# A two-layer graph attention kernel: three PSUM banks for the edge sums, scores two groups behind, softmax one slot later

## What is computed

```
def _egat_conv(x, e, src, dst, W_ni, W_nj, W_fij, W_node, attn):
    f = (x @ W_ni.T)[src] + (x @ W_nj.T)[dst] + e @ W_fij.T
    f = leaky_relu(f, negative_slope=0.2)
    score = f @ attn
    m = segment_max(score, dst)
    a = exp(score - m[dst])
    a = a / segment_sum(a, dst)[dst]
    h = x @ W_node.T
    return segment_sum(h[src] * a[:, None], dst), f

h0, h1 = _egat_conv(x, e, src, dst, ...W1...)
h0 = relu(h0) + x
h1 = relu(h1) + e
h0b, _ = _egat_conv(h0, h1, src, dst, ...W2...)
out = layernorm(x + h0b + x)
```

## Time and profile before

| what | us |
|---|---|
| median of 3 runs | 2160.43 (2159.26 to 2163.89) |
| the profiled execution | 2163.74 |
| its span, first to last instruction | 2162.0 |
| PE busy | 1872.9 (87%) |
| POOL busy | 1593.5 (74%) |
| DVE busy | 1351.5 (63%) |
| ACT busy | 672.6 (31%) |

### The profile page before, as it was taken

How to read it: one execution, slowest core, us unless ns; L and a number is a source line. 1 busy time by engine, 2 the same in 40 slices (tenths; PEclk the granted TensorE clock), 3 DMA queues, 4 the chain that set the end, 5 groups by cost and what they waited for, 6 DMA issues and landing times.

```text
span 2162.0 us, 41030 instructions
## 1 busy us (share of the span) xinstructions
PE 1872.9 (87%) x10816; PEld 1284.3 (59%) x10816; DVE 1351.5 (63%) x4574; ACT 672.6 (31%) x1260; POOL 1593.5 (74%) x1664
## 2 busy tenths in 40 slices
PE   5799999898888899898978998888888888888887
PEld 4366766566565666566756666565555555565656
DVE  6477776665665666665745756656556556555655
ACT  2555444443433434443211112222222222122221
POOL 7777777777777777777577777777777777777771
PEclk9899999989999989988989989989999999989998
DMA  9888898888888888888756776666766766766761
GB/s 321 261 269 287 281 290 268 255 259 253 262 256 254 262 247 266 261 252 252 228 163 181 216 203 199 207 198 195 207 191 201 204 197 197 205 190 199 204 195 41
DMA packets 352481, 490.63 MB, mean 227 GB/s; under 512 B 115219, under 2 KB 217924, under 8 KB 352092
## 3 DMA queue, kind: packets, MB, share of 16 engines
q1 hardware_dynamic: 236803, 249.78, 38.0%
q0 software_dynamic: 78416, 212.69, 33.4%
q10 hardware_dynamic: 37017, 25.40, 3.9%
HBM read 409.00 MB, written 81.38 MB: 227 GB/s over the span
## 4 chain that ended last, share of the span: by engine, by line
PE 41%; DMA 23%; issue 12%; POOL 9%; DVE 7%; ACTq 6%; ACT 2%; POOLq 0%; DVEq 0%; SPq 0%
DMA xsrc<-h_table,idx_slot 11%; PE bSC L935 9%; DMA xsrc<-x_table,idx_slot 9%; POOL xsrc L612 9%; PE pair L946 9%; PE pair L894 8%; PE pair L915 7%; ACTq L778 4%; PE pair L919 3%; ACTq L774 2%; DVE fT L1419 1%; DMA proj<-xsrc 1%; ACT zc L738 1%; PE bX L1000 1%; DVE amat L1267 1%
## 5 line engine op out<-in xcount | busy, mean ns | idle before, releaser
L612 POOL DMA_INDIRECT xsrc<-h_table,idx_slot x804 | 777.1, 967 | 246.9 <-issue 201.3
L612 POOL DMA_INDIRECT xsrc<-x_table,idx_slot x767 | 730.8, 953 | 233.8 <-issue 194.2
L738 ACT ACTIVATE zc<-pair 128x512 f32<-128x512 f32 x416 | 248.4, 597 | 1334.4 <-PE pair L919 1137.7
L1419 DVE TENSOR_TENSOR fT<-pair,zc 128x512 f32<-128x512 f32 x416 | 286.1, 688 | 350.9 <-ACT zc L738 348.1
L894 PE MATMUL pair<-edge_in,wts 128*128 128x512 f32 x832 | 488.3, 670 | 10.3 <-DMA window<-proj 10.3
L915 PEld LDWEIGHTS pair<-ident,xsrc 128*128 128x128 f32 x1600 | 204.8, 152 | 472.1 <-DMA xsrc<-h_table,idx_slot 213.6
L935 PE MATMUL bSC<-fT,attn_at 128*32 128x128 f32 x3328 | 478.9, 291 | 3.7 <-DVE fT L1419 3.7
L946 PEld LDWEIGHTS pair<-amat,xsrc 128*128 128x128 f32 x3328 | 432.8, 201 | 64.1 <-issue 50.6
L946 PE MATMUL pair<-amat,xsrc 128*128 128x42 f32 x3328 | 465.2, 293 | 2.2 <-DVE amat L1269 2.0
L915 PE MATMUL pair<-ident,xsrc 128*128 128x128 f32 x1600 | 275.1, 299 | 191.7 <-DMA xsrc<-h_table,idx_slot 119.5
L935 PEld LDWEIGHTS bSC<-fT,attn_at 128*32 128x32 f32 x3328 | 350.2, 116 | 113.9 <-issue 92.0
(11 more groups left out here) (169 smaller groups left out, 1407.5 us busy)
## 6 DMA issues: line engine op xcount, KB each, us to landing
edge_in<-eT SPq DMA_DIRECT2D x208, 256.0 KB
rel_bc<-relrow_g SPq DMA_DIRECT2D x416, 128.0 KB
h1T<-h SPq DMA_DIRECT2D x208, 256.0 KB
edge_in<-h1T SPq DMA_DIRECT2D x208, 256.0 KB
stage<-h_table ACTq DMA_DIRECT2D x896, 1.0 KB
window<-proj SPq DMA_DIRECT2D x416, 32.0 KB
xsrc<-h_table,idx_slot POOLq DMA_INDIRECT x824, 3.7
xsrc<-x_table,idx_slot POOLq DMA_INDIRECT x767
```

The lines of the kernel that those rows point to most:

```text
L612: pool.indirect_dma_start(xsrc[b][:, i, 0:width], None, table, bass.IndirectOffsetOnAxis(ap=idx_slot[b][:, i:i + 1], axis=0)).then_inc(L.g ...
L738: nc.scalar.mul(zc[s][:, :], bZ[s][:, :], SLOPE).then_inc(L.z_scaled, 1)
L1419: v.tensor_tensor(fT[s][:, :], bZ[s][:, :], zc[s][:, :], ALU.max).then_inc(L.f_made, 1)
```

## The change

- z gets a third bank: the bank `bXT`, from group 16 on. `zc` and `fT` get a third buffer. Waits for the bank's last reader reach three groups back in place of two, from group 19 on (`apart`).
- In slot n PE makes the scores of group n - 2 (before: n - 1).
- In turns 0 to 25 every softmax step comes one slot later (`later` gives 1), and `partial`, `add_sums` and `weighted_onehot` follow one slot later too (`LAG` = 14).
- In the drain turns (c at least 26) `later` gives 0 and the lag is 13 as before. To catch up, slot 208 does two of each: `lags(26, 0)` is [14, 13]. PE also makes two groups of scores there.
- The slab sum goes to bank `bX2`, which the transposes and the products use too (slabs below 24). `slab_sum` moves to g = 7, the transposes to g = 0 and the products to g = 2 of the next turn; ScalarE's and VectorE's slab steps in layer 1 follow at g = 1, 3, 4 and 5. At turn 26 transposes and products of slab 23 both run at g = 0. New waits: the sum waits for the slab before to be wholly through the bank, and the products wait for ScalarE's copy of the rows.

The core of the diff:

```
-LAG = GC + 5
+LAG = GC + 6
+def bank_of(narrow, n, g):
+    if not narrow:
+        return g % 2
+    return (n - 2 * GC) % 3 if n >= 2 * GC else n % 2
+def apart(narrow, n):
+    return 3 if narrow and n >= 2 * GC + 3 else 2
+def later(c):
+    return 0 if isinstance(c, int) and c >= CH else 1
+def lags(c, g):
+    if not isinstance(c, int) or c < CH:
+        return [LAG]
+    return [LAG, LAG - 1] if (c, g) == (CH, 0) else [LAG - 1]
...
-        bZ = [p[:, 0:W] for p in pair]
+        bZ = [p[:, 0:W] for p in pair] + [bXT[:, :]]
...
 z_sum (PE)
-                    above(pe, L.f_made if L.h1_out is None else L.h1_made, n - 1)
+                    above(pe, L.f_made if L.h1_out is None else L.h1_made, n - apart(narrow, n) + 1)
...
 turn (PE)
-                        if g == 0:
-                            if soft:
+                        if g < 2:
+                            if soft and g <= d:
+                                scores(c - 1, GC - 2 + g)
+                            if soft and d == 0 and g == 0:
                                 scores(c - 1, GC - 1)
                         elif front:
-                            scores(c, g - 1)
+                            scores(c, g - 2)
...
-                            if g == 6:
+                            if g == 6 + d:
                                 slab_sum(c - 2, (c - 1) * GC)
-                            if g == 7:
+                            if g == 7 and d == 0:
                                 slab_rest(c - 2)
-                        if not (isinstance(c, int) and not 0 <= n - LAG < NG):
-                            late = g < LAG - GC
-                            partial(c - 2 if late else c - 1, (g - LAG) % GC, (b - (2 if late else 1)) % XB)
+                        if narrow and 3 <= c <= CH:
+                            if g == 0:
+                                slab_turned(c - 3)
+                            if g == 2 * d and L.n == 1:
+                                slab_product(c - 3)
+                        for lag in lags(c, g):
+                            if not (isinstance(c, int) and not 0 <= n - lag < NG):
+                                late = g < lag - GC
+                                partial(n - lag, (g - lag) % GC, (b - (2 if late else 1)) % XB)
...
 turn (DVE)
-                        if due(n - LAG - 1):
-                            add_sums(n - LAG - 1, (g - LAG - 1) % 2, nodes[g])
...
-                        if due(n - LAG + 1):
-                            weighted_onehot(n - LAG + 1, (g - LAG + 1) % GC, True)
+                        for lag in lags(c, g):
+                            if due(n - lag - 1):
+                                add_sums(n - lag - 1, (g - lag - 1) % 2, nodes[n - lag - 1] if narrow else None)
...
+                        for lag in lags(c, g):
+                            if due(n - lag + 1):
+                                weighted_onehot(n - lag + 1, (g - lag + 1) % GC, True)
...
-                            if g == 0:
+                            if g == d:
                                 row_maxima(c - 1)
```

More of the change, by code:

```diff
@@ L356, in slabs, with sum_bank, rows_bank @@
                 body(m, m % 2, m % 4, m // 4)
+        def sum_bank(k, narrow):
+            return bX2 if narrow and k < CH - 2 else bXT
+        def rows_bank(L, k, narrow):
+            return bX2 if L.n == 2 or narrow and k < CH - 3 else bXT
         def reached(m, first):
@@ L731, in slot @@
                     n, s = c * GC + g, g % 2
+                    z, d = bank_of(narrow, n, g), later(c)
                     ahead_made = L.n == 1 and front and not (isinstance(c, int) and n == NG - 1)
@@ L736, in slot @@
                         act.wait_ge(L.z_made, n + 1)
-                        above(act, L.f_made, n - 1)
-                        nc.scalar.mul(zc[s][:, :], bZ[s][:, :], SLOPE).then_inc(L.z_scaled, 1)
+                        above(act, L.f_made, n - apart(narrow, n) + 1)
+                        nc.scalar.mul(zc[z][:, :], bZ[z][:, :], SLOPE).then_inc(L.z_scaled, 1)
                     if ahead_made:
                         one_hot(c, g + 1)
-                    if g == 0 and soft:
+                    if g == d and soft:
                         act.wait_ge(L.score_made, c * GC)
@@ L973, in slab_sum @@
                     pe.wait_ge(L.num_added, added)
-                    if L.n == 1:
+                    if narrow and k < CH - 2:
+                        above(pe, L.low if L.n == 1 else L.out_made, k)
+                        if L.n == 2 and k == 0:
+                            pe.wait_ge(L1.low, CH)
+                    elif L.n == 1:
                         above(pe, L.rows_copied, k)
@@ L1028, in turn @@
                     fill = FILL if isinstance(c, int) and c == CH else {}
+                    d = later(c)
                     for g in range(GC):
@@ L1382, in turn @@
                     due = lambda n: not static or 0 <= n < NG
-                    begin = c * GC - LAG - 1
-                    if static and not due(begin):
-                        skip = min(GC, max(0, -begin))
-                    else:
-                        skip = 0
-                    count = min(GC - skip, NG - begin - skip) if static else GC
-                    nodes = [None] * GC
-                    if narrow and count > 0:
-                        nodes = [None] * skip + list(first_nodes(group_row, begin + skip, count)) + [None] * GC
-                    elif not narrow and due(c * GC - GC):
-                        nodes = [None] * (GC - 2) + list(first_nodes(group_row, c * GC - GC, 1)) + [None]
+                    d = later(c)
+                    nodes = {}
+                    if narrow:
+                        sums = [c * GC + g - lag - 1 for g in range(GC) for lag in lags(c, g)]
+                        sums = [m for m in sums if due(m)]
+                        if sums:
+                            nodes = dict(zip(sums, first_nodes(group_row, sums[0], len(sums))))
                     for g in range(GC):
-                        n, s, q = c * GC + g, g % 2, g % GS
+                        n, z, q = c * GC + g, bank_of(narrow, c * GC + g, g), g % GS
                         if not one and front and not (static and n == NG - 1):
```

115 lines of the change are left out of this document (69 added, 46 removed).

## The result

| | median us | lowest to highest, runs |
|---|---|---|
| before, beside the changed kernel | 2163.54 | 2159.26 to 2165.7, 5 |
| changed | 2176.72 | 2175.0 to 2182.0, 5 |
| changed / before | 1.0070 | 95% interval 1.0055 to 1.0084 |

A forecast was written before the change was run, and what follows sets the result against it. POOL's back-to-back gathers were taken to bound both layers, PE waiting for them. Start 0.6, crossing 3.9 and end 4.0 summed to +8.5 us on 2160.4, giving 2168.9, rounded 2169 us (chance 67%); range 2161 to 2176.

The forecast's parts named there:

- Gathers set the pace, third bank 0: Both layers: POOL's gathers set the time, so third bank, third buffers and later scores bring 0 (ends 0 and -10.5 us).
- Crossing, "+4.05 us, row_maxima": Layer 1 to 2: row_maxima waits behind the doubled sums and one-hots of slot 208, +4.05 us; +3.9 in the sum.
- The 0.2 us that the sum took off for a shorter slot 207: Crossing: slab sum 23 no longer stands ahead of z(207), taken as 0.2 us won.
- So the delay passes on whole.: Crossing: from slot 209 orders and lags equal the old ones, so the delay reaches layer 2's start undiminished, +3.9 us.
- Start, "+0.6 us": Start of layer 1: group 24's gather waits for group 0's sums, made a slot later; +0.6 us (ends 0 and 2.5).
- Layer 2, 0: Inside layer 2: all shifts by the same amount, waits near group 40 stay; 0 (ends -1.4 and +3 us).
- End, "+4.0": Drain after layer 2: the crossing's queue without products makes row_maxima later, +4.0 us (ends 1.2 and 6).
- Slab steps, 0: Inside the layers: moved slab steps have a slot of about 5 us and POOL does not wait for them; 0.
- A: Drains: slot 208's catch-up is absorbed, only PE's longer queue counts; +2.1 us, 2162.5 us, no visible change; chance 15%.
- D: Whole kernel: the wide branch is taken, so the change is not run; 2160.4 us; chance 3%.
- B: Layers: PE's pace counts and the third bank removes its waits for f; faster, 2150.6 us; chance 6%.
- C: Inside the layers: PE falls behind POOL's lead at say ten places, or low clock is commoner; +7, 2176 us; chance 9%.

The follow-up runs named there:

- two banks: Changed kernel with z, zc and fT back on two banks and two buffers in both layers; 1.0072 of before on chip F, 2857.38 us on chip B.
- changed (G): The changed kernel, unaltered, run again on chip G beside the kernel before; 2179.62 us against 2163.56, ratio 1.0084.
- experiment 5: Kernel before and changed kernel, both unaltered, run again on one chip, G; 1.0002 for before, 1.0084 for changed.
- run of both: As early, and the softmax of chunk 0 in its old slots with lag 13 in turns 0 and 1; 2171.98 us against 2167.4 before, 1.0018.
- experiment 3: The run two banks: changed kernel with two banks and two buffers; on chip B 2857.38 us against 2824.43 changed, POOL waiting 217.6 us for f against 152.8.
- early: Changed kernel with softmax and lag back in their old places from turn 25, not slot 208; 2168.0 us on chip G against 2163.56 before, 1.0018.

## Why the prediction was wrong, step by step

The direction and the places were right; 2176.7 lies above the forecast of 2169 and just above the range. Of the 7.8 us between them 3.1 are the base: the forecast built on 2160.43, the median of three executions, and five gave 2163.54. The other 4.7 are the change's, 13.2 us where 8.5 were forecast. Its steps:

- *Gathers set the pace, third bank 0.* Right, shown by two banks (F). The scores two behind were not tried apart; the run with two banks had two buffers as well and still no wait near group 40, so the 1.8 us there belong to another part of the change, the later scores or the later sums, which was not found out.
- *Crossing, "+4.05 us, row_maxima".* The mechanism is shown. Measured 3.65 us in each of eight readings (8.01 or 8.00 less 4.36; 7.14 less 3.50), and 0.21 after the order was restored (4.57), 1.07 at the end. Of the 0.4 us too many 0.25 came from the one-hot matrices, 0.61 and not 0.74 us each, 0.10 from PE's queue and 0.05 from the step to the sum. The 0.2 us that the sum took off for a shorter slot 207 did not come: the last z copy is 4.93 and 5.35 us behind the last gather in before, 5.16 and 5.08 in changed.
- *"So the delay passes on whole."* This is the step that failed. It holds at the upper clock: changed (G) has 36.12 us behind `row_maxima` at the end, as before has 36.12. But with the late order the clock fell within 8 us behind `row_maxima` in four of six drains with fillers and in both without; in none of the eight with the old or restored order, all with fillers (there it falls some 20 us behind, where the work runs out). The chips of 2800 us repeat it: seven of eight drains with the late order and fillers, none of eight restored. That added 2.1 to 4.0 us to each drain with fillers that fell (at the crossing by the argument of experiment 5; 36.97 to 38.56 against 34.8; 40.14 against 36.1). What PE did ahead of it: with partial(194) done it waited 1.2 us for one-hot 195, busy 2.81 us of 4.00. That idle time stands in every drain with the late order, also in those that kept the clock, and in none of the others is PE idle above 0.4 us in the 4 us ahead of `row_maxima`. That the order brings the falls is shown by the runs; that it does so by this idle time fits all of them but was not tried apart. I had the half clock as an end of the range (6 us for each drain) and not in the sum. With VectorE's list of sum and two one-hots before me, I priced the wait for `row_maxima` and not PE's own wait for the first one-hot, nor what may follow from it.
- *Start, "+0.6 us".* Mis-sized: +2.4 and +2.2. By the working the first partial would end at 127.1 us; it ended at 128.82 and 128.05. Of the 1.97 us that I let PE win by work left out, it won 129.06 - 128.82 = 0.24 in the first pair (on G 0.43). In the first pair the first z itself was made 1.05 us later (75.45 us, before 74.40), which may be part of the 1.73 us that are missing; the rest stays open. From the partial's end to the gather it took 0.91 us and not 0.80. The end of 2.5 us was nearer. The run of both shows that POOL's wait goes with the order of turn 1. The two figures agree by luck in part, since two executions of this order differ by 2 us here.
- *Layer 2, 0.* -1.8 by the change, the rest of the first pair's 7.1 is a difference in the gathers' own duration, which hid 5.3 us of the loss in that pair. In layer 1 it went the other way (from the 97th gather on 700.5 to 702.8 us busy in six profiles with changed orders, 699.4 and 700.2 in two of before), and whether the change has a part in this 1 to 2 us stays open.
- *End, "+4.0".* +3.6 at the upper clock, +7.2 at the lower.
- *Slab steps, 0.* Not tried apart; from the 97th gather on none inside the layers waits more than 0.33 us in any of the six profiles of a changed order, so they cost nothing there.

Put right, the sum is: start 2.3, crossing 3.65 and the clock 3.1 (mean of 3.7, 2.1 and 3.6), end 3.64 and the clock 1.3 (4.0 in one of three with fillers), layer 2 -1.8: 12.2 us. The terms are read off the same profiles, so this is an account and not a test: the profiles show 11.3 (with the 5.3 us of quicker gathers in it) and 12.0. The medians differ by 13.2 us in the first pair and by 16.1 on G, where the profiled execution, 2174.1 us, was the shortest of four; what the longer executions did no profile shows.

**Rivals.** A falls: `row_maxima` moved by its 3.65 us and not by 0.3. D falls: the narrow branch ran, the sums are 42 columns wide. B rested on a rule of the Trainium skill (Perfetto Trace Analysis, Optimization Strategy: a gap repeating on the engine that should be saturated can mean too few buffers). On the chips of 2165 us the runs disagree, 1.0072 with two banks and 1.0070 with three; on those of 2800 us, where POOL stands waiting for f by the numbers of experiment 3, they agree, with 33 us. C's time, 2176, is all but the measured one, and that is chance: its mechanism, POOL waiting inside the layers, did not occur (no idle time above 0.33 us there). For it I had named the Trainium skill's section on PSUM-queue cycling (TensorE: Matmul & The Clock Gate, A second HAM failure mode: psum-queue depth-cycling), which lets short idle times of TensorE between groups set off a swing of the clock. The banks did nothing of this: 0.96 and 0.94 in layer 2 with three, 0.95 with two (F), 0.93 and 0.95 before. But a short idle time of PE ahead of a fall is what the drains show, in six of eight cases, though as a single one and not as a cycle.

No version beats the kernel before where the gathers set the pace: early and both stand 0.2% above it. On the chips of 2800 us early and both lie at 0.9985 to 1.0065.

## What to carry to other kernels

Where one engine sets the pace in the middle, a change of the order is paid or won only in the drains, so look there for what must catch up, and put the catching up where the pacing engine still covers it: that one move took 11.6 of the 16.1 us back (medians of ten and four executions on chip G). When a delay makes the tensor engine wait in a stretch with no cover, as the 1.2 us did here, price the clock as well, with its chance. And compare two profiles only after a second profile of the same kernel: 5.3 of the 7.1 us that layer 2 seemed to win were the same gathers running a little faster, with no such difference in the second pair.

## What the runs showed of the hardware, unexpected

The three chips of 2800 us ran every kernel 27 to 31% slower, and not because instructions take longer: a gather has a median of 946 to 949 ns there, 946 or 947 here. What stands out is that other engines start late behind TensorE. Timeline of changed on chip B: the last matmul of z loads its weights at 1599.94 (the record of the matmul itself is missing); TensorE has gone on to the scores at 1600.90 and to a partial at 1602.23, and only then, at 1602.34, does ScalarE start the copy it had been idle for (SyncE, waiting as well, starts a load at 1602.33):

```profile
1599.94 0.15 PEld L964 LDWEIGHTS pair<-onehot,window 128*128 128x128 bf16 x1
...
1600.90 1.40 PE L981 MATMUL bSC<-fT,attn_at 128*32 128x128 f32 x8
...
1602.23 1.09 PE L992 MATMUL pair<-amat,xsrc 128*128 128x42 f32 x8
1602.33 0.33 SPq L478 DMA_DIRECT2D edge_in<-h1T  x1
1602.34 0.60 ACT L775 ACTIVATE zc<-pair 128x512 f32<-128x512 f32 x1 [6.52 <-remote]
```

In the profile of before, ScalarE starts 0.04 us after that matmul's end in all but one (0.09 us) of some 320 cases in which it stood waiting; in before without fillers on chip A it is more than 0.5 us late in some 110 of 250, mostly by up to 9.6 us. There POOL is held up by TensorE and VectorE (in that run it waits 146.9 us for partials and 75.7 for f), and then a third bank pays against two in the changed order. What makes these starts late was not found. So a verdict on buffers can turn with the chip that the kernel meets.
